# A gated attention and feed-forward block: later values folded head by head, and two turnings issued from ScalarE's queue

## The reference

```python
x = x + tanh(g_xattn) * (softmax(q k^T / 8) v @ Wo + bo)   # q = layernorm(x) @ Wq, k, v = ctx @ Wk, ctx @ Wv
# feed-forward on n = layernorm(x), every linear layer on quantised data:
#   activations: round(x * 127 / max|row|), weights: clip(round(w / mean|w|), -1, 1)
g, u = bitlinear(n, w_gate), bitlinear(n, w_up)            # 512 -> 2048
x = x + tanh(g_ffn) * bitlinear(square(relu(g)) * u, w_down)   # 2048 -> 512
```

## Time and profile before

| | us |
|---|---|
| time, median of 3 runs (lowest to highest) | 1190.67 (1190.2 to 1194.57) |
| time of the profiled execution | 1190.42 |
| its span, first to last instruction | 1188.6 |
| PE busy | 1174.0 (99%) |
| DVE busy | 1033.9 (87%) |
| ACT busy | 869.2 (73%) |
| POOL busy | 307.2 (26%) |

### The profile page before, as it was taken

The page is one execution under the profiler, slowest core; times in us unless marked ns, Lnnn a source line. Parts: engine busy times, 40 slices in busy tenths (PEclk is TensorE's granted clock), DMA queues, the critical chain, the costliest instruction groups (busy, mean ns, idle before and its releaser), DMA issues.

```text
span 1188.6 us, 18855 instructions
## 1 busy us (share of the span) xinstructions
PE 1174.0 (99%) x5867; PEld 744.8 (63%) x5867; DVE 1033.9 (87%) x2124; ACT 869.2 (73%) x929; POOL 307.2 (26%) x313
## 2 busy tenths in 40 slices
PE   9989999999999999999999999999999999999998
PEld 7656656665665666566566656666665666666554
DVE  4989898888988888888998888889899888988887
ACT  5877777776887677677877767776787777677764
POOL 3222222222442222222442222222244222222200
DMA  9793554444444464444444464443444444444333
GB/s 356 262 297 77 156 147 100 98 111 97 97 112 102 126 158 114 96 108 97 101 100 101 115 179 108 98 110 93 101 113 101 100 97 110 97 101 108 84 65 76
DMA packets 286485, 144.71 MB, mean 122 GB/s; under 512 B 254586, under 2 KB 255226, under 8 KB 283889
## 3 DMA queue, kind: packets, MB, share of 16 engines
q1 hardware_dynamic: 286445, 144.32, 47.7%
q10 hardware_dynamic: 4, 0.00, 0.0%
HBM read 57.86 MB, written 24.35 MB: 69 GB/s over the span
## 4 chain that ended last, share of the span: by engine, by line
PE 86%; DVE 7%; ACT 3%; issue 2%; DMA 1%; POOL 0%; DVEq 0%; ACTq 0%; POOLq 0%
PE gu_ps L1084 34%; PE o_ps L1048 17%; PE y_ps L1098 17%; PE s_ps L66 17%; DVE half_max L1330 1%; DVE staged L1324 1%; DMA staged<-in_wd_t 1%; PE gu_ps L1148 1%; PE gu_ps L1208 1%; DMA a_scr<-a_spare 0%; DVE w_up L1484 0%; DVE staged L1456 0%; ACT staged L778 0%; DVE w_down L1484 0%; ACT x_marked L854 0%
## 5 line engine op out<-in xcount | busy, mean ns | idle before, releaser
L1084 PE MATMUL gu_ps<-w_up,xq_t 128*128 128x512 bf16 x1024 | 241.9, 379 | 1.9 <-DVE staged L1324 1.9
L1084 PE MATMUL gu_ps<-w_gate,xq_t 128*128 128x512 bf16 x1016 | 240.9, 380 | 1.3 <-DMA xq_t<-xq 1.2
L1098 PE MATMUL y_ps<-w_down,hq_t 128*128 128x512 bf16 x1008 | 227.8, 379 | 0.0
L1048 PE MATMUL o_ps<-v_sb,pt_high 128*128 128x512 f32 (+1 forms) x640 | 212.8, 413 | 0.9 <-DVE pt_low L1313 0.9
L1324 DVE TENSOR_TENSOR staged<-staged,gu_ps 128x1024 f32<-128x1024 f32 x128 | 155.6, 1216 | 53.5 <-ACT staged L784 53.5
L66 PE MATMUL s_ps<-a_sb,xf_high 128*128 128x308 f32 x1024 | 187.4, 305 | 0.0
L1084 PEld LDWEIGHTS gu_ps<-w_up,xq_t 128*128 128x128 bf16 x1024 | 100.0, 98 | 123.6 <-DVE staged L1324 3.8
L645 POOL TENSOR_TENSOR rstd<-var_eps,neg_half 128x1 f32<-128x1 f32 x128 | 96.4, 753 | 307.1 <-DVE var_eps L1289 274.6
L824 ACT ACTIVATE staged<-staged,h_scale 128x1024 f32<-128x1024 f32 x126 | 137.9, 1142 | 48.9 <-DVE h_scale L1344 48.9
L1098 PEld LDWEIGHTS y_ps<-w_down,hq_t 128*128 128x128 bf16 x1008 | 98.8, 98 | 118.8
L778 ACT ACTIVATE staged<-gu_ps 128x1024 f32<-128x1024 f32 x127 | 128.9, 1015 | 52.4 <-PE gu_ps L1084 52.0
(11 more groups left out here) (146 smaller groups left out, 1438.8 us busy)
## 6 DMA issues: line engine op xcount, KB each, us to landing
xf_sb<-in_x_feat SPq DMA_DIRECT2D x64, 256.0 KB, 2.6
x_sb<-in_x_tok SPq DMA_DIRECT2D x64, 256.0 KB, 2.9
y<-staged SPq DMA_DIRECT2D x63, 256.0 KB, 2.0
staged<-in_wg_t SPq DMA_DIRECT2D x4, 1024.0 KB, 9.5
staged<-in_wd_t SPq DMA_DIRECT2D x4, 1024.0 KB, 7.6
folded<-a_scr SPq DMA_DIRECT2D x3, 1232.0 KB, 5.6
v_scr<-x SPq DMA_DIRECT2D x12, 256.0 KB
folded<-v_scr SPq DMA_DIRECT2D x3, 1024.0 KB, 5.1
```

The source lines that it names most:

```text
L1048: last = nc.tensor.matmul(o_ps[:, :], pt[0:rows, P * c:P * (c + 1)], v_sb[0:rows, v, c, :], start=(c == 0 and pt is pt_high and v == 0), s ...
L1084: last = nc.tensor.matmul(target[:, q, :], xq_t[:, s.par(0), c, :], w[:, c, cols], start=(c == 0), stop=(c == DC - 1))
L1098: last = nc.tensor.matmul(y_ps[:, :], hq_t[:, c, :], w_down[:, c, :], start=(c == 0), stop=(c == FC - 1))
```

## The change

**Values.** Batches 1 to 3 are no longer folded by batch but by head: all 231 later rows of one head, in two parts of 116 and 115 rows, 16 parts in all. A part lies within one head, so its contraction is the head's 64 rows, it is one matmul, and it needs no block form: the three later `place_values` go. The parts straddle batches, so each is stored by two DMAs, 32 instead of 15. `v_scr` becomes 617 plain rows per batch. There are seven SBUF places for values and three for keys.

**Queue of ScalarE.** `turn_first_input` and `turn_second_probs` issue the first input's and the second probabilities' transposes from ScalarE's list; SyncE waits for both before its steps.

**First piece of w_down.** Piece (2,0) is loaded into `v_pairs` as soon as batch 0's values are folded. It is clipped to plus or minus the unit on DVE, rounded and placed by two ScalarE operations; DVE's scale and ternary of it go.

**Orders.** All eight gate and up pieces are loaded up front; the loads of the second tile's features and of x follow behind the first key store. All five lists are written anew, and measures and scales change engines. In `first_step` DVE takes attention first.

```diff
+A_PLACE = [0, 1] * 5 + [0, 2]
+V_PLACE = [0, 1, 2, 3, 4, 0, 1, 2, 3, 4, 0, 1, 2, 3, 5, 6]
+FIRST_ROWS = ((BATCH - 1) * KEYS + 1) // 2
+def head_part(k):
+    h, s = divmod(k, 2)
+    return h, KEYS + FIRST_ROWS * s, FIRST_ROWS - s
+def part_runs(k):
+    _, first, rows = head_part(k)
+    r = 0
+    while r < rows:
+        b, j = divmod(first + r, KEYS)
+        n = min(KEYS - j, rows - r)
+        yield b, j, n, r
+        r += n
...
+                def store_later_values(k):
+                    at = KEYS * head_part(k)[0]
+                    sp.wait_ge(vo_taken, k + 1)
+                    for b, j, n, r in part_runs(k):
+                        sp.dma_start(v_scr[b, at + j:at + j + n, :].rearrange("p (q n) -> p q n", q=HP),
+                                     v_slots[V_PLACE[k]][r:r + n, :, :]).then_inc(v_stored[V_STORE[k]], 16)
...
+                def turn_first_input():
+                    act.wait_ge(xq_done, 1)
+                    act.dma_start_transpose(xq_t[:, 0, :, :], xq[:, :]).then_inc(xq_turned, 16)
+                def turn_second_probs():
+                    act.wait_ge(probs_left, 2)
+                    act.dma_start_transpose(planes_t[:, :, :], planes[:, :]).then_inc(probs_turned, 16)
...
+                def mark_first_down():
+                    act.wait_ge(unit_inv_done, 3)
+                    act.wait_ge(weight_stage[2][0], CLIPPED)
+                    nc.scalar.activation(raw(2, 0), raw(2, 0), ACT.Copy, bias=ROUND,
+                                         scale=inv_unit[:, 2:3]).then_inc(weight_stage[2][0], 1)
+                def place_first_down():
+                    act.wait_ge(weight_stage[2][0], LIFTED)
+                    act.wait_ge(weight_stage[1][0], SCALED)
+                    there = w_down[:, :, :].rearrange("p c n -> p (c n)")[:, 0:PIECE]
+                    nc.scalar.activation(there, raw(2, 0), ACT.Copy, bias=-ROUND).then_inc(weight_stage[2][0], 1)
...
+                def fold_later_values(k):
+                    h, first, rows = head_part(k)
+                    if k < V_RING:
+                        pe.wait_ge(v_split_done, KC + k - V_RING + 1)
+                    else:
+                        pe.wait_ge(vo_taken, k - V_RING + 1)
+                    own = slice(HEAD * (h % 2), HEAD * (h % 2 + 1))
+                    nc.tensor.matmul(value_slots[(KC + k) % V_RING][0:rows, :], v_t[own, h // 2, first:first + rows], wo_sb[own, h // 2, :],
+                                     start=True, stop=True, tile_position=(HEAD * (h % 2), 0)).then_inc(vo_done, 1)
...
+                def clip_first_down():
+                    nc.vector.tensor_scalar(neg_unit[:, :], unit[:, 2:3], -1.0, None, ALU.mult).then_inc(unit_done, 1)
+                    dve.wait_ge(unit_done, 4)
+                    dve.wait_ge(weight_stage[2][0], MEASURED)
+                    nc.vector.tensor_scalar(raw(2, 0), raw(2, 0), unit[:, 2:3], neg_unit[:, 0:1],
+                                            ALU.min, ALU.max).then_inc(weight_stage[2][0], 1)
```

More of the change, by code:

```diff
@@ L912, in step @@
                         mark_hidden(s, -1)
-                    if s.has(0):
+                    if s.has(0) and not s.opens(0):
                         relu_half(s, 0)
@@ L959, in _ @@
                 measure(0, 1)
+                first_values(0)
                 take_keys(1, 0)
-                measure(0, 2)
-                first_values(0)
+                measure(1, 2)
+                first_values(1)
+                measure(0, 3)
+                first_values(2)
+                exponentials(start, 0)
+                first_values(3)
+                scale(0, 3)
                 take_keys(1, 1)
-                exponentials(start, 0)
-                first_values(1)
+                first_values(4)
@@ new lines, in _ @@
+                high_part(start, 2)
+                measure(2, 0)
+                take_keys(3, 0)
+                take_later_values(8)
+                take_later_values(9)
+                mark_input(start, 0)
+                take_later_values(10)
+                take_keys(3, 1)
+                exponentials(start, 1)
+                take_later_values(11)
+                take_later_values(12)
+                turn_first_input()
+                measure(2, 1)
+                part_probs(start, 1)
@@ L1089, in down @@
                     if s.opens(-d):
[L1090 removed]
+                        wait(pe, weight_stage[2][0], PLACED)
+                        for p in range(1, PIECES):
                             wait(pe, weight_stage[2][p], DONE)
@@ L1640, in _ @@
+                shift_scores(start, 0)
+                sum_rows(0)
+                first_values_low(2)
+                find_unit(0)
+                first_values_low(3)
+                scale(0, 0)
+                sum_probs(start, 0)
+                first_values_low(4)
+                ternary(0, 3, w_gate)
                 dve.wait_ge(rstd1_done, 1)
                 input_stats(start, 1)
-                top_scores(start, 0)
-                shift_scores(start, 0)
-                split_bias()
@@ L1645, in _ @@
-                dve.wait_ge(tanh_done, 1)
-                first_values_low(0)
-                measure(0, 3)
-                first_values_low(1)
-                sum_probs(start, 0)
-                sum_rows(0)
-                first_values_low(2)
+                measure(1, 0)
+                sum_rows(1)
+                ternary(0, 0, w_gate)
+                scale(0, 1)
+                find_unit(1)
+                find_hidden_unit()
+                probs_low(start, 0)
+                ternary(0, 1, w_gate)
@@ L1652, in _ @@
+                ternary(0, 2, w_gate)
+                scale(1, 2)
+                scale(1, 0)
+                ternary(1, 3, w_up)
+                ternary(1, 0, w_up)
+                ternary(1, 1, w_up)
+                add_attention(start, 0)
+                input_scale(start, 0)
+                top_scores(start, 1)
+                shift_scores(start, 1)
+                unmark_input(start, 0)
+                sum_probs(start, 1)
+                ternary(1, 2, w_up)
                 dve.wait_ge(rstd1_done, 2)
@@ L1668, in _ @@
-                ternary(1, 3, w_up)
-                scale(1, 0)
-                ternary(1, 0, w_up)
-                top_scores(start, 1)
-                ternary(0, 3, w_gate)
-                scale(1, 1)
-                shift_scores(start, 1)
-                ternary(1, 1, w_up)
-                sum_probs(start, 1)
-                measure(2, 1)
-                add_attention(start, 0)
-                input_scale(start, 0)
+                measure(2, 2)
+                measure(2, 3)
+                sum_rows(2)
@@ L1683, in _ @@
                 hidden_unit_scale(start, 0)
-                sum_rows(2)
-                unmark_input(start, 0)
-                sum_probs(start, 2)
                 find_unit(2)
                 find_down_unit()
+                clip_first_down()
+                probs_low(start, 1)
                 scale(2, 1)
-                scale(2, 0)
-                ternary(2, 0, w_down)
-                probs_low(start, 1)
+                sum_probs(start, 2)
                 ternary(2, 1, w_down)
```

405 lines of the change are left out of this document (202 added, 203 removed).

## The result

Before: 1191.36 us, median of 20 runs (1189.48 to 1194.57). Changed: 1194.8 us, median of 20 runs (1189.96 to 1196.92). The ratio is 1.0024, with an interval of 1.0016 to 1.0032: about 3 us slower. The forecast was 1189.2 us, 2.2 under the median of before. The time lies inside the range of 1183.5 to 1195.0, at its top, and the direction was wrong.

A forecast was written before the change was run, and what follows sets the result against it. DVE's list was taken to bound the stretch ahead of 159 us, PE the steady steps. -1.5 us up to the first step and +0.3 in step 0 gave -1.2, so 1190.42 became 1189.2 us; range 1183.5 to 1195.0.

The forecast's parts named there:

- The bound: Whole kernel: steady steps bound by PE, 17.28 us each; ahead of 159 us DVE's list binds.
- TensorE's folds: Prologue on PE: 24 matmuls become 16 at 0.86 us each, 6.9 us less, changing the forecast by nothing.
- DVE's work and waits up to the unit: Prologue on DVE: work grows by 1.5 us; the walk with waits ends the hidden unit scale at 81.5.
- The chain through ScalarE: Late prologue: ScalarE's copies and issues, then PE's folds, end `total(2)` at 81.1; DVE reads the unit at 81.5.
- rival 1: Prologue: ScalarE's issues last until landing, 6.15 us on DVE's unit, 1195.4; decides above 4.1 us together; chance 0.08.
- dear issues: Prologue transposes holding ScalarE 1.63 and 2.66 us: DVE reads the unit at 82.6, gain 0.4 instead of 1.5.
- a faster PE alone gives nothing: Ahead of 159 us PE has slack, 4.94 us lost after its first gate matmul; DVE's list binds there.
- The rule on issuing engines: Prologue transposes: the issuing engine changes only sequencer time, so SP's time becomes ScalarE's; it spoke against the move.
- From the unit to the first step: Late prologue on DVE: 7.6 us of operations, through at 89.0 for 90.49, a gain of 1.5.
- SP's stores at nothing: Prologue on SP: 17 more stores at 0.4 to 0.6 us cost nothing; uncovered, a copy waits some 2 us.
- rival 3: Prologue and step 0: dearer issues and reordered step 0 eat the gain, 1190.3 to 1191.3, 1190.8 taken; chance 0.21.

The follow-up runs named there:

- six spares: Changed kernel with six 128x128 matmuls into unused PSUM columns on PE ahead of the last key fold, `fold_keys(3, 3)`: 1190.69 us, ratio 0.9996.
- both turnings by SP: Changed kernel with both prologue transposes issued by SP again, between its stores: 1194.49 us, ratio 1.0023.
- old order of step 0: Changed kernel with six spares and DVE's step 0 in its order of before the change: 1191.27 us, ratio 1.0002.
- the turning ahead of store 12: Changed kernel with both transposes issued by SP, the probabilities' transpose ahead of the store of value part 12: 1192.72 us, ratio 1.0007.
- the turning behind the copies: Changed kernel with ScalarE's second transpose issued behind `take_keys(3, 2)`, `high_part` and values 13: 1196.06 us, ratio 1.0036.

## Why the prediction was wrong

**The bound: right.** The steady part didn't change, and its start is set by the chain before 165 us. That start moved by 5.7 us and the profiled time by 6.5.

**TensorE's folds: right to be left out of the sum as work**, but a single price was wrong. A fold of 64 rows costs 1.04 us alone (two passes of 512 columns: 1.11 with their tail), not 0.86, and a key part behind it 1.24 us (45.74 to 46.98), not 1.05. Where two adjacent parts use different halves of the rows they overlap:
```profile
42.28 1.12 PE L1298 MATMUL gu_ps<-folded,v_t 64*115 64x512 f32 x4
```
That is the timeline of PE after: four passes in 1.12 us, where two alone take 1.11. The last two parts are of one head and so use the same half, and their four passes take 1.97 us with six spares (at 79.81). The Trainium skill, "TensorEngine Tiling (Array Packing)", section "Key Properties", says that different tiles can run their matmuls in parallel, and this row agrees.

**DVE's work and waits up to the unit: right, and in this execution 1 us short at the end.** Unit 0 at 36.75 (36.7 predicted), first ternary done 43.3 (42.8), unit 1 at 49.79 (49.8), x_scale 67.94 (67.7), hidden unit scale done 82.47 (81.5); with six spares 81.65.

**The chain through ScalarE: the step that failed**, in two terms. The first is the price of the issues, 1.2 and 1.35 us, taken because "all weights have landed by then". They measured 2.61 and 2.26, 4.87 in sum for 2.55. The first ran beside a key store that SP issued at 70.47. Beside the second SP issued nothing; its end kept a distance of some 8 us from the start of the first. The prediction priced the two as independent. Their sum is over the 4.1 us that rival 1 named as its point, though for another reason: an issue does not last until the landing. The view of DMA issues after, 0 to 92 us (median us to landing), beside the earlier trace rows:
```profile
xq_t<-xq ACTq DMA_TRANSPOSE x1, 10.8
planes_t<-planes ACTq DMA_TRANSPOSE x1, 5.9
```
10.8 us against 2.61, 5.9 against 2.26. For dear issues, 4.29 in sum, the prediction has the unit at 82.6; its own terms give 82.8 (81.1 and 1.74 more). With 0.58 more still it is 83.4.

The second term was missing. The unit came at 86.30, 2.9 later than that, and 2.90 is what PE's folds cost more at the lower clock, from the comparison with the six spares. That the two agree so closely is in part luck: smaller errors along the chain (the marking 0.4 later, for one) cancel. The prediction read that PE has slack and that "a faster PE alone gives nothing". That holds for a faster PE. It did not ask what 3.35 us without work would do to PE's speed afterwards, with the last folds, `total(2)` and so DVE's unit behind it. The count with a wait put into the kernel before (7 of 10) speaks for the wait by itself being enough, and the spares, which change nothing but the wait, took the 4.1 us back. Whether the 64-row folds take part is open: with them the clock also fell behind waits of 0.94 and 1.14 us (both turnings by SP; old order of step 0), and the kernel before kept it in its profile behind 1.56 us (at 79.39).

**The rule on issuing engines.** The change only moved time from SP to ScalarE, and in the changed order either queue costs it (1194.49 by SP, 1194.8 by ScalarE; 1192.72 by SP with the turning ahead of store 12). The Trainium skill, "DMA: Bandwidth & Descriptors", section "Issuing engines are not separate DMA queues", says that issuing from several engines saves only the time that an issue takes on its sequencer, and these runs agree. It calls that time usually small beside the transfer; here it was 2.61 us of 10.8 to the landing, 2.26 of 5.9 and, with the turning behind the copies, 4.54 of 11.9.

**From the unit to the first step: 8.33 us for 7.6** with the clock kept (82.13 to 90.46, six spares). A wait of 0.66 for ScalarE's high part had not been counted, and the last ternary operation took 1.59 for 0.69 beside a GpSimd operation of 2.10 (87.88), one collision more than the prediction gave. With the unit itself 0.6 later than 81.5, this ate the predicted gain of 1.5: 90.46 for 90.49.

**SP's stores at nothing: wrong by the same mistake.** In the kernel after they cost no copy a wait, but four of them held SP 4.03 us at 84.79. With the turning behind the copies the issue on ScalarE's queue grew beside such a group, and a copy waited 2.49 us for a key store, the case that the prediction put at 2 us.

**What the runs make of the rivals.** With its clock kept the change gives rival 3's case, the gain eaten: 1190.69 us with spares, 1190.5 in the four runs of 0.999, for 1190.8. With the clock lost it lies at rival 1's 1195.4, by a mechanism that no rival named; the nearness is luck. The two groups differ by 1195.0 - 1190.5 = 4.5 us, with 16 runs of 20 in the slower; that makes the result. The 4.5 may hold more than the clock, as a longer issue also makes the wait longer: in the two profiles compared, the folds at the lower clock are 2.90 of 4.58. No version that ran beats the kernel before by more than its interval.

## What to carry to other kernels

An engine with slack is safe to delay only if what comes after the delay runs as fast as before: look for a stretch in which TensorE would have nothing to do, and price what stands behind it at half the clock as a case of its own. A DMA issue on a computing engine's queue is to be priced from the dearest issue seen beside the same traffic, not from the cheapest in a quiet step, and two issues on one queue together: moving the start of the second forward need not move its end. Look at the mean clock of every execution ahead of the medians: a median that moves by 0.3% may be a count of two groups. Then ask in a trace where the clock fell: off the critical path, as with the old order of step 0, a low mean cost next to nothing.

## What the runs showed of the hardware

- The granted clock after 3.35 us without a matmul fell to 0.50 for some 9 us of busy PE. For the same program the mean over the execution was low in 16 of 20; with 3.45 us in the kernel before, in 7 of 10. It also fell behind a wait of 0.94 us in one kernel where 1.03 us left it alone in another. What decides between executions stays open.
- The issue of one 16-bit transpose held its queue from 1.19 us to 4.54 us. Of two on ScalarE's queue the second ended 7.9 to 8.5 us after the start of the first in six kernels, with its own start 4.6 to 6.6 us after that. What it waits for no row shows; the longest on ScalarE's queue stood beside four value stores that held SP for 4.52.
- Two f32 passes of 64 rows cost 1.11 us; four, in the two halves of the rows, 1.12; four in the same half 1.97.
